# Softmax rows left unnormalised, their inverse sums sent through DRAM and multiplied into the mix

## The reference

```python
q, k, v = jnp.einsum('bsx,xMnd->Mbnsd', x, qkv)
a = jnp.einsum('bnsd,bntd->bnst', q, k) * q.shape[-1] ** (-0.5)
...
bias = jnp.where(rel >= 0, cum[:, jnp.clip(rel, 0)], PAD)
a = jax.nn.softmax(a + bias, axis=-1)
mix = jnp.einsum('bnst,bntd->bnsd', a, v)
return jnp.einsum('bnsd,ndx->bsx', mix, out_w)
...
x = _layernorm(x + _L0_attn_ref(x, ...), axis=-1)
x = _layernorm(x + _L0_ffn_ref(x, ...), axis=-1)
```

## Time and profile before

| | |
|---|---|
| median of 3 runs (lowest, highest) | 1304.31 us (1304.12, 1305.85) |
| the profiled execution's own time | 1305.56 us |
| its span | 1303.8 us |
| busy PE, PEld | 1120.3 us (86%), 782.4 us (60%) |
| busy DVE, ACT, POOL | 842.9 us (65%), 743.1 us (57%), 886.4 us (68%) |
| DMA queue of SP | 166.98 MB, 53.6% of 16 engines |
| granted PE clock over the span | 0.968 |

### The profile page before, as it was taken

One profiled execution on the slowest core, in us unless ns is written; L12 is line 12 of the kernel. 1 busy time (PEld: TensorE's weight loads), 2 busy tenths in 40 slices (PEclk: granted clock), 3 DMA queues, 4 the chain that ended last, 5 costly groups with the idle time before them and its releaser, 6 DMA issues.

```text
span 1303.8 us, 21982 instructions
## 1 busy us (share of the span) xinstructions
PE 1120.3 (86%) x6909; PEld 782.4 (60%) x6909; DVE 842.9 (65%) x2505; ACT 743.1 (57%) x1857; POOL 886.4 (68%) x527
## 2 busy tenths in 40 slices
PE   5424999999999999999999999999999999999985
PEld 3313666666666666666666666666666666666664
DVE  1411666666666676777776767767667777676756
ACT  2312666666666565665665656656556665565632
POOL 1432878777777677877666777776677777666740
PEclk9666999999999999999999999999999999999997
DMA  5776555555554555665545556554554665544710
GB/s 144 167 85 147 132 132 131 128 118 124 142 121 123 128 136 132 152 147 117 140 120 134 130 142 151 135 123 119 139 142 122 150 152 132 117 119 123 207 45 19
DMA packets 104353, 168.38 MB, mean 129 GB/s; under 512 B 10656, under 2 KB 66352, under 8 KB 104240
## 3 DMA queue, kind: packets, MB, share of 16 engines
q1 hardware_dynamic: 104240, 166.98, 53.6%
HBM read 41.63 MB, written 24.64 MB: 51 GB/s over the span
## 4 chain that ended last, share of the span: by engine, by line
PE 62%; DVE 16%; issue 8%; DMA 6%; ACT 6%; SPq 2%; DVEq 0%; POOL 0%; ACTq 0%
PE ps_o L933 20%; PE ps_t L917 15%; PE ps_rows L903 12%; PE ps_m L878 6%; DMA bias_by_distance<-x_t 6%; DVE prob L613 4%; DVE pt L630 4%; PE ps_m L947 3%; PE ps_m L883 3%; ACT pt L480 2%; DVE mix_sb L636 2%; DVE k_lo L599 1%; ACT prob L469 1%; DVE q_lo L599 1%; DVE shift L680 1%
## 5 line engine op out<-in xcount | busy, mean ns | idle before, releaser
L421 POOL TENSOR_SCALAR prob<-prob,inv 128x128 f32<-128x128 f32 (+7 forms) x512 | 879.2, 1728 | 369.5 <-DVE inv L620 367.4
L469 ACT ACTIVATE prob<-prob,low 128x128 f32<-128x128 f32 (+7 forms) x512 | 395.2, 773 | 140.7 <-DVE low L613 138.4
L613 DVE CUSTOM_DVE_ANT_0 prob<-ps_rows,table 128x128 f32<-128x128 f32 (+7 forms) x512 | 383.3, 749 | 134.8 <-PE ps_rows L903 106.4
L903 PE MATMUL ps_rows<-stacks 128*128 128x512 f32 (+3 forms) x1536 | 403.7, 373 | 64.4 <-DMA stacks<-k_lo 41.7
L917 PE MATMUL ps_t<-ident,prob 128*128 128x128 f32 x2304 | 349.9, 279 | 86.4 <-ACT pt L480 49.1
L917 PEld LDWEIGHTS ps_t<-ident,prob 128*128 128x128 f32 x2304 | 261.0, 141 | 198.2 <-issue 130.9
L903 PEld LDWEIGHTS ps_rows<-stacks 128*128 128x128 f32 x1536 | 247.2, 191 | 83.0 <-DMA stacks<-k_lo 41.9
L630 DVE COPY pt<-ps_t 128x256 f32<-128x256 f32 (+2 forms) x320 | 178.9, 567 | 180.5 <-PE ps_t L917 179.4
L480 ACT ACTIVATE pt<-ps_t 128x128 f32<-128x128 f32 (+2 forms) x448 | 203.3, 476 | 152.1 <-PE ps_t L917 152.0
L933 PE MATMUL ps_o<-pt,v_pair 128*64 128x512 f32 (+3 forms) x1536 | 268.6, 492 | 0.0
L933 PEld LDWEIGHTS ps_o<-pt,v_pair 128*64 128x64 f32 x1536 | 101.8, 136 | 181.8 <-issue 172.3
(11 more groups left out here) (106 smaller groups left out, 561.4 us busy)
## 6 DMA issues: line engine op xcount, KB each, us to landing
stacks<-k_hi SPq DMA_DIRECT2D x124, 256.0 KB, 4.9
stacks<-k_lo SPq DMA_DIRECT2D x124, 256.0 KB, 4.9
stacks<-q_hi SPq DMA_DIRECT2D x62, 256.0 KB, 4.5
stacks<-q_lo SPq DMA_DIRECT2D x62, 256.0 KB, 4.8
mix_transposed<-mix_sb SPq DMA_DIRECT2D x62, 256.0 KB, 2.0
table<-bias_by_distance SPq DMA_DIRECT2D x64, 192.0 KB, 2.6
mix_tile<-mix_transposed SPq DMA_DIRECT2D x24, 512.0 KB, 5.0
w_cur<-in_L_attn_qkv SPq DMA_DIRECT2D x32, 192.0 KB, 3.3
```

The source lines that it names most:

```text
L421: nc.gpsimd.tensor_scalar(row, row, inv[:, r:r + 1], None, ALU.mult).then_inc(s_norm, 1)
L469: nc.scalar.activation(row, row, ACT.Exp, bias=low[:, r:r + 1], scale=-1.0, accum_out=total[:, r:r + 1]).then_inc(s_exp, 1)
L613: nc.vector.tensor_tensor_reduce(prob[:, r % PSLOTS, 0:width], ps_rows[:, score_at(r):score_at(r) + width], table[n % 2][:, h, SEQ - width ...
L903: ins = nc.tensor.matmul(ps_rows[:, at + c0:at + c1], q_st(h, n)[:, P * i:P * i + P], k_st(h, n, low_part)[:, c0:c1], start=(low_part == 0 ...
```

## The change

POOL no longer multiplies the rows. The unnormalised exponentials are transposed and mixed. Per step DVE inverts the sums in two calls of eight rows each (slots 5 and 12). PE transposes each group of eight inverses into the unused last quarter of a bank (banks 6 and 19, `INV_BANK`), DVE or ACT copies the 8x128 result to `inv_t`, SP stores it to DRAM (`inverse_sums`), waits until it has landed there, and loads it back into `inv_all`, copied to the 64 partitions of each head (two transfers). `store_mix` on DVE then multiplies the mix by `inv_all` where it copied before.

```diff
+INV_READY = (5, 12)
+INV_BANK = (6, 19)
...
+            def spread_inverse(n, g):
+
+                sp.wait_ge(s_inv_t[g], n + 1)
+                sp.dma_start(inv_d[n % 2, g, :, :], inv_t[g][:, :]).then_inc(s_inv_d[g], 16)
+                sp.wait_ge(s_inv_d[g], 16 * n + 16)
+                if n > 0:
+                    sp.wait_ge(s_o, 2 * n + g)
+                for h in range(2):
+                    sums = inv_d[n % 2, g, GROUP * h:GROUP * h + GROUP, :].rearrange("(a i) q -> a (i q)", a=1)
+                    sp.dma_start(inv_all[g][D * h:D * h + D, :], sums.broadcast_to([D, GROUP * P]))\
+                        .then_inc(s_inv_all[g], 16)
...
                 if prev:
                     store_mix(n - 1, 1)
+                spread_inverse(n, 0)
                 if more:
                     sp.wait_ge(s_lo, 4 * n + 8)
...
                 store_mix(n, 0) if more else None
+                spread_inverse(n, 1)
...
-                nc.gpsimd.tensor_scalar(row, row, inv[:, r:r + 1], None, ALU.mult).then_inc(s_norm, 1)
...
+                if n > 0 and r % (2 * GROUP) == 0:
+                    act.wait_ge(s_inv, 2 * n - 1 + r // (2 * GROUP))
...
+                if k == INV_BANK[1]:
+                    if n > 0:
+                        act.wait_ge(s_inv_d[1], 16 * n)
+                    nc.scalar.activation(inv_t[1][:, :], ps_t[k % 2][0:2 * GROUP, 3 * P:], ACT.Copy).then_inc(s_inv_t[1], 1)
...
-            def invert(n, r):
-                dve.wait_ge(s_exp, NROWS * n + r + 1)
-                nc.vector.reciprocal(inv[:, r:r + 1], total[:, r:r + 1]).then_inc(s_inv, 1)
+            def invert(n, g):
+                rows = slice(2 * GROUP * g, 2 * GROUP * (g + 1))
+                dve.wait_ge(s_exp, NROWS * n + 2 * GROUP * (g + 1))
+                if n > 0:
+                    dve.wait_ge(s_tr, NBANKS * n + INV_BANK[g] + 1)
+                nc.vector.reciprocal(inv[:, rows], total[:, rows]).then_inc(s_inv, 1)
...
+                if k == INV_BANK[0]:
+                    if n > 0:
+                        dve.wait_ge(s_inv_d[0], 16 * n)
+                    nc.vector.tensor_copy(inv_t[0][:, :], ps_t[k % 2][0:2 * GROUP, 3 * P:]).then_inc(s_inv_t[0], 1)
...
-                nc.vector.tensor_copy(mix_sb[g][:, :], ps_o[:, :]).then_inc(s_o, 1)
+                dve.wait_ge(s_inv_all[g], 32 * n + 32)
+                nc.vector.tensor_tensor(mix_sb[g][:, :], ps_o[:, :], inv_all[g][:, :], ALU.mult).then_inc(s_o, 1)
...
-                pe.wait_ge(s_norm, NROWS * n + r + 1)
+                pe.wait_ge(s_exp, NROWS * n + r + 1)
...
+                    if k in INV_BANK:
+                        g = INV_BANK.index(k)
+                        pe.wait_ge(s_inv, 2 * n + g + 1)
+                        ins = nc.tensor.transpose(ps_t[k % 2][0:2 * GROUP, 3 * P:],
+                                                  inv[:, 2 * GROUP * g:2 * GROUP * (g + 1)], ident[:, :])
```

More of the change, by code:

```diff
@@ L94, in build @@
     mix_d = nc.dram_tensor("mix_transposed", (PAIR_STEPS, P, SEQ), F32, kind="Internal").ap()
+    inv_d = nc.dram_tensor("inverse_sums", (2, 2, 2 * GROUP, P), F32, kind="Internal").ap()
     xt_d = nc.dram_tensor("x_transposed", (BATCH, P, SEQ), F32, kind="Internal").ap()
@@ L130, in build @@
         inv = sb("inv", [P, NROWS])
+        inv_t = [sb(f"inv_t{g}", [2 * GROUP, P]) for g in range(2)]
+        inv_all = [sb(f"inv_all{g}", [P, GROUP * P]) for g in range(2)]
         pt = [[sb(f"pt{h}{g}", [P, GROUP * (g + 1), GROUP * P]) for g in range(2)] for h in range(2)]
@@ L202, in build @@
         s_inv = sem("inverted")
-        s_norm = sem("normalised")
+        s_inv_t = [sem(f"inverse_transposed{g}") for g in range(2)]
+        s_inv_d = [sem(f"inverse_in_dram{g}") for g in range(2)]
+        s_inv_all = [sem(f"inverse_broadcast{g}") for g in range(2)]
         s_tr = sem("transposed")
@@ L415, in _ @@
             pool.memset(one[:, :], 1.0).then_inc(s_zero, 1)
[L417 to L420, removed]
-                nc.gpsimd.tensor_scalar(row, row, inv[:, r:r + 1], None, ALU.mult).then_inc(s_norm, 1)
-            for n in range(PAIR_STEPS):
-                for r in range(NROWS):
-                    normalise(n, r)
             for w in range(TILES // WIDE):
@@ L700, in _ @@
                 bias(0, r)
-                if r:
-                    invert(0, r - 1)
             def step(n, prev, tile_too, more):
@@ L707, in step @@
                         bias(*row)
-                    for row in rows_ahead(n, more, slot - 1):
-                        invert(*row)
+                    if slot in INV_READY:
+                        invert(n, INV_READY.index(slot))
                     if more and slot in PROJ_SLOTS[:4]:
```

## The result

| | median us (lowest to highest) | runs |
|---|---|---|
| before | 1305.08 (1304.12 to 1306.07) | 4 |
| after | 1325.32 (1321.72 to 1326.44) | 4 |

The ratio is 1.015, with a 95% interval of 1.0128 to 1.0172. The time lies in the stated range, on the side that had the largest chance (slower, 0.47), but 20 us from the predicted 1305.7.

The account below looks back on a forecast made before the run. The chain lay 62% on PE, which idled some 3 us a step, at banks DVE and ACT copy late. Terms -3.7 + 0 + 1.2 + 0.5 + 3.4 = +1.4 gave 1307.0, as a median 1305.7 us; range 1299 to 1334.

Parts of the forecast that it names:

- The step that failed: SP's second round trip, behind the near mix: only transfers with consumers over 10 us away follow it, so no cost.
- late k halves and `mix_tile`: Rival, slot 12 and the next step's slot 0: transfers come late, 28 us in all, about 1334 us; chance 0.24.
- The first trip: SP's round trip ahead of the k halves: mostly hidden by slack, with 0.5 us in all added for late transfers.
- D: Delay of the k transfers behind SP's first round trip: 1.95 us, between 0.95 and 4.1.
- the idle time at row 14: PE's 0.68 us wait in a tile step, counted on for an earlier start and to take up 0.54 us of delay.
- L680: DVE instruction in the chain to `mv`: may take 0.29 us instead of 0.63; half of 7.5 us taken, -3.7 us.
- The start: PE's wait for the first k halves, where no slack exists: +3.4 us, once.
- POOL's products off the path: Taking POOL's products off the rows' path gives nothing by itself; POOL was 3.0 us ahead at row 14.
- rival 3: POOL did hold PE, in its weight-load waits: up to 60 us would go, 1246 us; chance 0.03.
- PE's transposes and the small copies: Two extra PE transposes a step and ACT's small copy: hidden in tile steps, 0.15 us in others, +1.2 us.
- DVE's inversions: 512 inversions become 64; between -0.2 and +0.2 us ahead of row 9, taken as 0.
- The sign of being wrong: The prediction is wrong if idle times at rows 9, 13 and 14 shrink by more than 0.34 us together.

Follow-up runs that it names:

- e1: The changed kernel with the load of the next batch's x issued ahead of the second round trip in three steps; 1311.63 us.
- e4: The kernel before, POOL's products kept, with only SP's two round trips a step added, their data unused; 1328.98 us.
- e10: The changed kernel with only the second round trip issued by POOL, the first left in SP's queue; 1312.80 us.
- e2: The changed kernel with both round trips of the inverse sums issued by POOL in place of SP; 1299.14 us.
- e3: The changed kernel without the round trips, the mix multiplied by a tile set to ones, so the output is not normalised; 1299.93 us.
- e8: The changed kernel without round trips, output not normalised, with POOL given 512 products on a tile of its own; 1300.66 us.

## Why the prediction was right and where it was wrong

**The step that failed** is the sentence that the second round trip "has only the tile's store and the next step's table and weights behind it, whose consumers are over 10 us away". In three steps of 32 the load of the next batch's x stands there too, with a consumer in slot 2 of the next step. It was in the code (`load_x_transposed`), but not in the step whose order I had read, and I had not gone through the queue for what comes only once in eight steps. The three steps are 16.4 of the 20 us longer, and e1, e4 and e10 each show it: PE waits 8.3 us for x, the lower clock behind adds 6.5, and 1.4 are `mix_tile`'s. That the range and the likeliest direction held is mostly luck: their slower part was made for late k halves and `mix_tile`, and what filled it was a load that the prediction does not name.

**The second trip's landing** was never worked out. It can be the longer one: 4.8 us from issue to issue at 628.83, where it queues behind the last k transfers, `mix_tile` (512 KB) and the near mix; the first has only the mix store ahead. At the first boundary, which has no output tile, it took 1.52 us (330.40 to 331.92), and x was late even so.

**The clock** was no term of the sum at all. At the second boundary L902 and the far mix took 2.04 and 5.77 us, for 1.10 and 3.65 in the kernel before: 3.1 us together, nearly as much again as the wait of 3.29. Over the three boundaries it is 6.5 us behind 8.3 us of waits.

**The first trip**: mechanism right, size too small. SP's delay is 1.55 us against 1.35. The loads' bytes and the crowding add 1.3 us where I had taken 0.6 (and 1.25 as the bound), so D is 2.8 and not 1.95 in the step read above, beyond the 2.25 to 2.4 at which I had said that it decides. The step read is the one with PE's longest wait for k halves; the others are milder. Outside the start and the three boundaries the late transfers cost 6 to 9 us: that much more time do the changed kernel, e10 and e1 take there than e2 (6.1, 7.5 and 9.3 in the profiled executions). A part of it is in the `mix_tile` waits, 3.5 us in nine [L976 of the changed kernel]. And the prediction used the idle time at row 14 twice, once for L680's relief and once to take up D. e4 shows the difference: without the relief, D costs the ordinary tile steps 1.1 us, and with it 5.2 (changed kernel against e2) to 7.0 (e1 against e2).

**The start**: 3.4 us predicted; PE goes on at 118.14 where it was 115.16, 3.0 us. In the five runs with the same order it goes on between 118.01 and 119.70, so the term is 2.9 to 4.5 us.

**L680**: I took half of 7.5 us. It came back nearly whole: row 14 starts 0.31 us earlier in e3, and most tile steps take 37.13 us against 37.46. In the changed kernel itself the late transfers hide it. The Trainium skill (SBUF — State Buffer, "Who interferes with whom") was nearer to it than my halving, in that the two engines do interfere on such operands. But it says that the later instruction is blocked until the other has ended, and here it is not so: POOL's product of row 15 takes 2.8 us and the DVE instruction grows by 0.10 to 0.34.

**POOL's products off the path** (rival 3, 60 us in PE's weight-load waits): right that they gave nothing. The same list now has 56.0 us of that row's kind for ACT's exponentials in place of POOL, so the time did not go with POOL's work: the row named a semaphore beside the one that counted.

**PE's transposes and the small copies**: 0.15 us a step without a tile predicted, 0.06 to 0.09 in e2 and e3 (34.47 and 34.50 against 34.41). Hidden in tile steps, as said. **DVE's inversions**: nothing, as said; row 9 starts where it did.

**The sign of being wrong** that I had set, over 0.34 us less idle time at rows 9, 13 and 14 together, was badly put. It is 0.52 us in e3, but 0.22 of that is the two new transposes, which fill idle time and move no row. A row's start, counted from a fixed point of the step, is the better sign.

## What to carry to other kernels

A wait put into an issuing queue must be checked against everything that is issued behind it in *any* iteration, the rare transfers first: a load that comes once in eight steps made two thirds of this loss or more. A small transfer whose landing the queue waits for took longer with bulk traffic ahead of it, 1.8 us at one place here and 4.8 at another; on the queue of an engine that is idle anyway (here POOL, freed by the same change) the same transfers cost nothing, and the change becomes a gain of 0.5%. An idle stretch on TensorE cost nearly twice its length here (2.03 us and 1.8 more, 3.29 and 3.1 more), so it should be costed with the granted clock behind it. A piece of idle time can take up a delay or give a gain, but not both.

## What I had not expected of the hardware

- After 3.29 us without work PE ran the next 2 us at a granted clock of 0.50 and the following 5.8 at 0.63. After 2.03 us its next products took 1.10 us, as usual, but the far mix behind them 5.33 us in place of 3.65: the granted clock there was 0.50 from 339 to 341.
- The same 8x128 store and load in one queue took 1.52, 1.83, 4.23 or 4.83 us from issue to issue, by what was ahead.
- POOL at work on a tile of its own lengthened a 128x128 DVE instruction on two SBUF operands from 293 to 386 and 396 ns, which began while a POOL instruction of 2.85 us was running.
- With the same work on POOL the TENSOR_SCALAR that writes `o_tile` (128x128, SBUF to SBUF, two columns of scalars) went from a median of 346 ns (L696 in e3) to 520 (L708 in e8); it was 522 in the kernel before (L686).
